# GpSimd adds all nine taps in three of four channel groups, and its stages run in another order

## What is computed

```python
def _L0_conv_ref(inputs, w_in, b_in, dw_kernel, dw_bias, ln_gamma, ln_beta, w_off, b_off, w_mask, b_mask, w_out, b_out):
    x_proj = inputs @ w_in + b_in
    x1 = ... # depthwise 3x3 convolution, layer norm, gelu
    offset = (x1 @ w_off + b_off).reshape(B, H, W, G, K2, 2)
    mask = jax.nn.softmax((x1 @ w_mask + b_mask).reshape(B, H, W, G, K2), axis=-1)
    ...
    samp = _bilinear_gather(xg, pxf, pyf, Hp, Wp).reshape(B, G, H, W, K2, GC)
    maskg = mask.transpose(0, 3, 1, 2, 4)
    out = jnp.sum(samp * maskg[..., None], axis=4)
    out = out.transpose(0, 2, 3, 1, 4).reshape(B, H, W, C)
    return out @ w_out + b_out
...
x = x + _L0_conv_ref(_ln_c(x), ...)
t = t + _L0_ffn_ref(_ln_t(t), ...)   # router, top 2 of 8 experts, 64 -> 256 -> 64
```

## Time and profile before

| what | value |
|---|---|
| median of 3 runs | 315.28 us (314.25 to 315.37) |
| span of the profiled execution | 312.6 us |
| what lies around the span (median less span) | 2.7 us |
| busy: TensorE, ScalarE, VectorE, GpSimd | 278.6, 257.1, 240.5, 122.1 us |
| chunk 0, chunk 1, chunk 2 | about 36 to 91, 91 to 159, 159 to 227 us |
| last chunk, and what follows it | about 227 to 290, 290 to 312.6 us |

### The profile page before, as it was taken

The page is one execution under the profiler, slowest core; times in us unless marked ns, Lnnn a source line. Parts: engine busy times, 40 slices in busy tenths (PEclk is TensorE's granted clock), DMA queues, the critical chain, the costliest instruction groups (busy, mean ns, idle before and its releaser), DMA issues.

```text
span 312.6 us, 8542 instructions
## 1 busy us (share of the span) xinstructions
PE 278.6 (89%) x3312; PEld 179.4 (57%) x3312; DVE 240.5 (77%) x720; ACT 257.1 (82%) x495; POOL 122.1 (39%) x123
## 2 busy tenths in 40 slices
PE   7977898968799998899999997999979999998895
PEld 2552476635467654445667663444667787776562
DVE  6999769999957987679878887498958354479565
ACT  3878679899796999989796999988868899887473
POOL 5230151504452705031584413050966713569230
PEclk9999999999999999999999999999999999999999
DMA  6910000000000000000000000000000000000000
GB/s 143 306 37 0 3 2 4 0 2 2 0 3 2 4 2 0 2 0 3 2 9 13 2 0 0 3 2 1 2 19 0 3 2 2 10 1 12 2 0 17
DMA packets 7189, 4.84 MB, mean 15 GB/s; under 512 B 5089, under 2 KB 6830, under 8 KB 7086
## 3 DMA queue, kind: packets, MB, share of 16 engines
q1 hardware_dynamic: 7150, 4.31, 5.7%
HBM read 2.04 MB, written 0.52 MB: 8 GB/s over the span
## 4 chain that ended last, share of the span: by engine, by line
PE 43%; DVE 23%; ACT 18%; issue 9%; POOL 6%; DMA 1%; DVEq 0%; ACTq 0%; POOLq 0%
ACT wk L1284 5%; PE zl_ps L1533 5%; ACT wk L1279 4%; PE ga_ps L1564 3%; PE zh_ps L1530 3%; PE m_ps L1666 3%; PE ga_ps L1566 3%; PE ga_ps L1565 3%; DVE wx L851 3%; DVE prod L863 3%; PE m_ps L1649 2%; ACT h_all L1315 2%; PE m_ps L1507 2%; DVE samp L878 2%; PE m_ps L1452 2%
## 5 line engine op out<-in xcount | busy, mean ns | idle before, releaser
L863 DVE TENSOR_TENSOR prod<-ga_ps,wx 128x480 f32<-128x480 f32 x96 | 61.9, 651 | 30.3 <-PE ga_ps L1566 29.5
L547 POOL TENSOR_TENSOR prod<-prod 128x960 f32<-128x960 f32 (+1 forms) x20 | 39.8, 1991 | 111.6 <-DVE prod L863 111.6
L1279 ACT ACTIVATE wk<-zh_ps 128x512 f16<-128x512 f32 x108 | 65.3, 604 | 21.7 <-PE zh_ps L1530 20.6
L1564 PE MATMUL ga_ps<-v_all,wk 128*128 128x80 f16 x576 | 79.2, 201 | 4.0 <-DVE prod L863 1.4
L1566 PE MATMUL ga_ps<-v_all,wk 128*128 128x80 f16 x576 | 79.2, 202 | 0.0
L1565 PE MATMUL ga_ps<-v_all,wk 128*128 128x80 f16 x576 | 79.1, 201 | 0.0
L1564 PEld LDWEIGHTS ga_ps<-v_all,wk 128*128 128x128 f16 x576 | 56.5, 98 | 17.1 <-issue 6.3
L1284 ACT ACTIVATE wk<-zl_ps 128x512 f16<-128x512 f32 x108 | 65.6, 607 | 0.0
L1565 PEld LDWEIGHTS ga_ps<-v_all,wk 128*128 128x128 f16 x576 | 57.0, 99 | 7.8
L1566 PEld LDWEIGHTS ga_ps<-v_all,wk 128*128 128x128 f16 x576 | 57.2, 99 | 0.0
L1533 PE MATMUL zl_ps<-tab,sel_lo 128*128 128x512 f16 x108 | 41.6, 385 | 7.0 <-ACT wk L1284 4.4
(11 more groups left out here) (283 smaller groups left out, 622.2 us busy)
## 6 DMA issues: line engine op xcount, KB each, us to landing
v_all<-still SPq DMA_DIRECT2D x1, 1440.0 KB, 9.9
h_all<-in_W SPq DMA_DIRECT2D x1, 512.0 KB
w_s<-in_W SPq DMA_DIRECT2D x1, 512.0 KB
x_tok<-in_x SPq DMA_DIRECT2D x1, 384.0 KB, 6.4
out_dram<-x_tok SPq DMA_DIRECT2D x6, 64.0 KB, 1.7
w_high<-w_high SPq DMA_DIRECT2D x1, 256.0 KB, 2.9
const<-in_table SPq DMA_DIRECT2D x1, 218.0 KB, 2.6
vec<-in_vectors SPq DMA_DIRECT2D x1, 132.5 KB
```

The costliest lines, as they stand in the source:

```text
L547: then(pool.tensor_tensor(p[:, 0:3, :], p[:, 0:3, :], p[:, 3:6, :], ALU.add))
L863: dve.tensor_tensor(prod[q % 2][:].rearrange("p k n -> p (k n)")[:, f * PB * NV:(f + 1) * PB * NV] .rearrange("p (n c l) -> p n c l", n=PB ...
L1279: act.activation(wk[n % WR][:, 0, :], zh_ps[:], ACT.Relu, scale=W_SCALE).then_inc(s_wkh, 1)
L1564: pe.matmul(to, w_h, high, start=True, stop=False)
```

## The change

In quarters 0, 1 and 2 of a full chunk (half quarters 0, 1, 2, 4, 5 and 6 of the last one) GpSimd now adds all nine taps: `tap_tree` keeps its first add alone, and a new stage `tap_rest` waits for all fills of the quarter, adds planes 6 to 8 and then the three planes into plane 5. VectorE then sums only the five lanes of plane 5, in one reduction for the whole quarter. In quarter 3 (half quarters 3 and 7) all stays as it was.

```diff
+def by_tree(j, q):
+    return q % Q != Q - 1
...
                 then(pool.tensor_tensor(p[:, 0:3, :], p[:, 0:3, :], p[:, 3:6, :], ALU.add))
+                if not by_tree(j, q):
+                    then(pool.tensor_tensor(p[:, 0, :], p[:, 0, :], p[:, 1, :], ALU.add))
+                    pool.tensor_tensor(p[:, 5, :], p[:, 0, :], p[:, 2, :], ALU.add).then_inc(s_tap, 1)
+
+            def tap_rest(j, q):
+
+                if j < LAST:
+                    pool.wait_ge(s_ga_rd, FILLS * j + FQ * (q + 1))
+                    p = prod[q % 2]
+                else:
+                    pool.wait_ge(s_ga_rd, FILLS * j + HALF_FQ * (q + 1))
+                    p = half_prod(q)
+                then(pool.tensor_tensor(p[:, 0:3, :], p[:, 0:3, :], p[:, 6:9, :], ALU.add))
                 then(pool.tensor_tensor(p[:, 0, :], p[:, 0, :], p[:, 1, :], ALU.add))
                 pool.tensor_tensor(p[:, 5, :], p[:, 0, :], p[:, 2, :], ALU.add).then_inc(s_tap, 1)
...
+                if by_tree(j, q):
+                    if half == 0:
+                        dve.tensor_reduce(samp[:, 0:TP, 2 * q:2 * q + 2, :].rearrange("p t g c -> p t c g"),
+                                          prod[q % 2][:, 5, :].rearrange("p (t c g l) -> p t c g l", t=TP, c=GC, g=2),
+                                          axis=AX.X, op=ALU.add).then_inc(s_samp, 1)
+                    return
...
+                        if by_tree(j, q) and n == at["tap_rest"][q]:
+                            tap_rest(j, q)
```

The tables of places change on GpSimd, and on VectorE for the sums alone. The line for the last chunk:

```diff
-POOL_LAST = {"tap_tree": [4, 22.5, 29.5, 44, 45.5, 56.5, 67, 71.5], "combine": [34, 63.5], "conv_rstd": 30.5,
+POOL_LAST = {"tap_tree": [6, 15, 24, 33, 42, 51, 60, 69], "tap_rest": [9.5, 18.5, 27.5, 0, 45.5, 54.5, 63.5, 0], "combine": [34, 63.5], "conv_rstd": 30.5,
```

More of the change, by code:

```diff
@@ L64 @@
              "conv_norm": 10.5, "image_out": 10.5, "positions": [14.5, 17, 16.5], "rows": [17.5, 19.5, 20.5, 22],
-             "edges": 15, "hats": 25, "tap_weights": [22, 25], "lane_sum": [9.5, 9.5, 17.5, 17.5, 27, 28, 0, 3],
+             "edges": 15, "hats": 25, "tap_weights": [22, 25], "lane_sum": [13, 0, 22, 0, 31, 0, 0, 3],
              "residual": 4.5, "inner_norm": 12, "zn_low": 2, "route": [4, 13, 14.5], "expert_weights": 14.5, "b2": 14,
@@ L68 @@
              "second_stats_": 0, "second_norm": 0}
-POOL_FIRST = {"tap_tree": [4.5, 5, 23.5, 29.5], "combine": [35.5, 22.5], "conv_rstd": 4.5, "inner_rstd": 21.5,
-              "input_rstd": 28}
+POOL_FIRST = {"tap_tree": [4.5, 15, 23.5, 33], "tap_rest": [9, 18, 27], "combine": [35.5, 22.5], "conv_rstd": 4.5, "inner_rstd": 21.5,
+              "input_rstd": 19}
 PE_MIDDLE = {"input_t": 0, "convolve": [4, 6, 7, 7], "project": 5, "image_t": [9, 12.5], "conv_t": 14, "offsets": 15.5,
@@ L80 @@
               "image_out": 12.5, "positions": [13.5, 17.5, 14], "rows": [19, 22.5, 25, 30], "edges": 26.5, "hats": 21,
-              "tap_weights": [29.5, 32.5], "lane_sum": [9, 16.5, 19.5, 22.5, 26.5, 28.5, 0, 0], "residual": 3,
+              "tap_weights": [29.5, 32.5], "lane_sum": [13, 0, 22, 0, 31, 0, 0, 0], "residual": 3,
               "inner_norm": 4.5, "zn_low": 8.5, "route": [11.5, 13, 18.5], "expert_weights": 19.5, "b2": 16.5,
               "bias_rows": 4.5, "router_parts": 12.5, "w1_low": [8, 9.5, 11, 17], "outputs_in": [34, 35]}
-POOL_MIDDLE = {"tap_tree": [18.5, 21, 22.5, 35.5], "combine": [35.5, 35.5], "conv_rstd": 19.5, "inner_rstd": 17.5,
-               "input_rstd": 18.5}
+POOL_MIDDLE = {"tap_tree": [5, 15, 23.5, 33], "tap_rest": [9.5, 18, 27], "combine": [35.5, 35.5], "conv_rstd": 6, "inner_rstd": 3.5,
+               "input_rstd": 12}
 PE_LAST = {"input_t": 7.5, "convolve": [4.5, 9, 15.5, 21], "project": 0, "image_t": [11.5, 25], "conv_t": 24.5,
@@ L100 @@
             "half_inner_norm": 47.5, "half_zn_low": 56, "half_route": [57, 59, 67], "half_expert_weights": 68.5,
-            "lane_sums": [15, 21.5, 29.5, 44, 46, 61, 69.5]}
-POOL_LAST = {"tap_tree": [4, 22.5, 29.5, 44, 45.5, 56.5, 67, 71.5], "combine": [34, 63.5], "conv_rstd": 30.5,
+            "lane_sums": [14, 22, 31, 44, 48, 57.5, 66.5]}
+POOL_LAST = {"tap_tree": [6, 15, 24, 33, 42, 51, 60, 69], "tap_rest": [9.5, 18.5, 27.5, 0, 45.5, 54.5, 63.5, 0], "combine": [34, 63.5], "conv_rstd": 30.5,
              "inner_rstd": 0, "input_rstd": 47, "half_inner_rstd": 46, "router_exp": 22, "half_router_exp": 66}
@@ L890, in lane_sum_last @@
                     dve.wait_ge(s_sT, LAST)
+                if by_tree(LAST, i):
+                    dve.tensor_reduce(samp[:, half * TH:(half + 1) * TH, 2 * q:2 * q + 2, :].rearrange("p t g c -> p t c g"),
+                                      half_prod(i)[:, 5, :].rearrange("p (t c g l) -> p t c g l", t=TH, c=GC, g=2),
+                                      axis=AX.X, op=ALU.add).then_inc(s_samp, 1)
+                    return
                 for t in range(TH):
```

## The result

The changed kernel takes 325.06 us (median of 4 executions, 324.39 to 325.87), the kernel before 314.79 us (4 executions): a ratio of 1.0315, with a 95% interval of 1.0287 to 1.0342 (the two medians alone give 1.0326). Its profiled execution spans 323.7 us where the one of before spans 312.6. The 11.1 us between them are what has to be found.

The account below looks back on a forecast made before the run. VectorE bounds chunk 0, TensorE and ScalarE in turns chunks 1 and 2, GpSimd the last chunk's end. Span 312.6 + 5.6 + 3.0 + 1.2 = 322.4 us, with 2.7 us around it 325 us; range 318 to 330.

Parts of the forecast that it names:

- Term one, the queue at the end: End of last chunk: GpSimd's longer queue delays VectorE's last sum by 5.6 us, bounds 2.4 and 7.
- two added adds make 2.4 of it, the hole the rest: GpSimd's end in the last chunk, 5.5 us later: 2.4 from two added adds, the rest from idling before half quarter 6.
- Term two, the held operations: GpSimd's adds hold up VectorE operations: 3.0 us in chunks 1 and 2, 1.2 us in chunk 0.
- The way through ScalarE: Chunk 1: clamps and cells held, uloc ends at 129.7, ScalarE waits about 1.5 us; chunk 2 alike.
- the upper bound: Chunks 1 and 2: 5 us, if edges behind quarter 2's tap_rest makes the next chunk's table late too.
- the middle term: Chunks 1 and 2: held VectorE operations cost 3.0 us together, bounds 0 and 5.
- the relief: Chunk 0, quarters 1 and 2: VectorE sums removed on the chain, worth 2.4 us.
- a rival beside the forecast: TensorE's clock falls to 1.2 GHz in the gap before the last samples_t: 3 us more, 328 us; chance 0.2.
- The 2.7 us around the span: Time outside the profiled span, added to the forecast span of 322.4 us to give 325 us.
- The queue alone: Stalls vanish in VectorE's idle time and chunk 0's saving pays for them; only 5.6 us at the end: 321; chance 0.17.
- Faster: VectorE's relief decides, at 57 to 85 us and the end of chunk 2, -1 at last chunk: 312; chance 0.07.
- no change: The relief and a tail of only 2.4 us cancel: 315 us; chance 0.06.

Follow-up runs that it names:

- run 8: Changed kernel with combine and the exponentials again ahead of half quarter 6's trees, its sum behind expert_weights, added adds kept; 322.81 us.
- run 7: Kernel before, with only combine and the exponentials moved behind half quarter 6's tree and that half quarter's sum ahead of expert_weights; 319.24 us.
- run 6: Changed kernel's order of stages with the arithmetic of the kernel before, so no added adds; 320.59 us.
- runs 4 and 3: Kernel before with added adds and new order in chunks 1 and 2 alone (4), 316.81 us, or in chunk 0 alone (3), 316.09 us.
- run 5: Changed kernel without the wide first add of tap_rest, leaving three of nine taps out in those groups; 317.83 us.
- run 9: Changed kernel with combine ahead of half quarter 6's tree and the exponentials between its first add and its tap_rest on GpSimd; 325.51 us.
- run 1: Changed kernel with the last chunk's sums and order put back as before, the first three chunks keeping the added adds; 318.15 us.

## Why the prediction was right, and where its terms were off

The forecast of 325.0 us meets the measured 325.06, in part because errors cancel.

**Term one, the queue at the end (5.6 us).** Measured 4.8. Its rows came as foreseen: `combine` at 290.81, which is 286.6 on the clock of before (287.0 foreseen), a hole ahead of half quarter 6, and the last add and the last sum's end 4.9 and 4.8 us late. Of the 0.8 us too much, 0.3 is half quarter 6's tree, which began at 282.96 on that clock and not at 283.3, and 0.3 the last product and sum, which lie closer together than I had them. The split was wrong in its reason, not in its sum: "two added adds make 2.4 of it, the hole the rest" takes them as costs that add. In nearly the old order the adds make 2.9 us (run 8), the move of `combine` alone 2.7 (run 7), the whole changed order without the adds 4.3 (run 6), and on top of that order the adds cost just 0.4 us, because they lie in the hole.

**Term two, the held operations (3.0 us in chunks 1 and 2, 1.2 us in chunk 0).** Measured by the lowest executions 2.2 and 1.3 (runs 4 and 3), and 3.4 together against 4.2. The mechanism stands: a VectorE operation of this kind that meets a wide add lasts until it ends (2.33, 2.36, 2.47 us), and with the wide add gone it doesn't (run 5). The way through ScalarE was only in part right. In chunk 1 `uloc` came 4.6 us later and ScalarE started on it 3.0 us later, but the next wide tree began only 2.10 us later (139.69 against the earlier trace rows), of which 2.05 were chunk 0's. What cost there was `edges` behind quarter 2's `tap_rest`, which I had only in the upper bound: `edge` held for 1.9 us and `xn` for 0.5 us, on a stretch in which the chain of waits runs through VectorE (from 144.72 us on, where the one of before lies on TensorE and ScalarE). That is read from the chain; no run took `edges` apart from the clamps. So the place of the middle term was missed, and its size was 0.8 us too high. In chunk 0 the relief was worth 1.5 us against before and 2.1 us against run 6's order (run 5), where I had 2.4.

**The cost that was left out: TensorE's clock.** I had this as a rival beside the forecast, at 3 us and with a chance of 0.2. It happened (the mean clock was 0.974 to 0.984 in all four executions), and cost 2.1 us at the end and, in the profiled execution, some 0.7 us in chunk 0. The step that failed is the choice of the likeliest case: the gap that I foresaw came, 5.03 us long, and I held the fall behind it for the less likely, because no row of before showed one. The Trainium skill, TensorE: Matmul & The Clock Gate, section Why this matters for your kernels, warns of idle gaps between bursts of matmuls, behind which the clock is back at its lower level. This trace agrees: 0.50 behind the gap.

**The sum.** The three terms were 9.8 us and measured 8.3 (4.8, 2.2, 1.3); the clock left out was 2.8; so the span was 323.7 us and not 322.4. The 2.7 us around the span were wrong: they set the median of before against the span of another execution. In every execution on record that has both, span and time lie 1.7 to 2.0 us apart, here 1.8 (325.51 and 323.7). These three errors (1.5 too much, 2.8 too little, 0.9 too much) nearly cancel, and the median of four lies 0.4 us below the profiled execution. That the middle of the forecast was met to 0.1 us is luck; that the queue's cost and the held operations came as foreseen in kind is not.

**What was costed at nothing.** The moved `conv_rstd` and `input_rstd` cost nothing in sum (run 6: the half's `y_r` within 0.1 us of before, though chunk 0 ended 0.6 us later). The waits of the last chunk that went away, 4.7 us of them, gave nothing: between `y_r` of the last chunk and that of its half both kernels take 41.79 us.

**The rivals.** The queue alone (321) is out, by runs 3 and 4. Faster and no change are out; only the place for the first was right, chunk 0, where the relief shows once its price is left out.

**Open.** Why the clock falls in some executions of the same code in chunk 0 and chunk 2 and not in others isn't settled; a fall there was never forced or prevented in a run. That a nine-tap tree in quarter 2 of chunk 0 is a gain rests on lowest executions alone.

## What to carry to other kernels

Work given to an idle engine has two prices that its busy share doesn't show: the place in that engine's queue, and what it does to its neighbours while it runs; look first for what stands behind it in order at the place where the engine is waited for. Before a stage moves in one engine's queue, lay the other engine's order beside it: in run 9 filling a hole on GpSimd opened one on VectorE. Two delays at one place don't add up: price them together on the clock. And where a delay leaves TensorE without work, put the fall of its clock into the likeliest case.

## What the runs showed of the hardware

A GpSimd add of 960 elements per partition that is under way when one of these VectorE operations on SBUF operands comes holds it until the add's end: a clamp of 0.30 us became 2.33, `uloc` of 0.45 us 2.47, `edge` of 0.46 us 2.36. A 320-wide add did the same for its own 1.0 us (run 5: 0.97). Not everything is held: products with one operand in PSUM kept their 0.65 us beside it, and in the kernel before a sum over taps (two reductions, 0.87 us at 119.70, inside the add from 119.09) kept its time too. It also goes the other way round: an add that began at 155.64, inside VectorE's `wx` operation (155.48, 1.65 us), took 3.57 us where most take 2.2.

With the change or without it, TensorE's clock falls in some executions and not in others of the same code: chunk 0 of the changed kernel shows 0.63 and 0.52 from 68 to 76 us, and 1.00 in run 1. The kernel before took from 314.3 us at a mean clock of 1.000 to 316.7 us at 0.983. Behind a gap of 5.03 us TensorE worked 7.8 us at 0.50 before the clock came back (windows 300 to 308), behind one of 3.48 us (run 7) the four us after it show 0.60 and the next 0.97, and behind one of 0.46 us the clock stayed.
